# The first stage of a fused two-layer network on one NeuronCore: another order of loads, statistics and roots

## What is computed

```python
x = x + fourier_conv(_ln_c(x))      # layer 0: DFT over axes 1 and 2 (channel, height), 32x32 kept modes,
                                    # a 64x64 complex matrix over the width for each mode, inverse DFT
t = tokens(x); t = t + top2_of_8_experts(_ln_t(t))
x = x + depthwise_29x29_conv(_ln_c(x))   # layer 1
t = tokens(x); t = t + top2_of_8_experts(_ln_t(t))

def _ln_c(v, eps=1e-06):            # normalises each pixel over its 64 channels
    m = mean(v, axis=1); s = var(v, axis=1)
    return (v - m) / sqrt(s + eps)
```

## Time and profile before

| what | value |
|---|---|
| time, median of 3 runs | 1081.36 us (1080.91 to 1082.05) |
| the profiled execution | 1083.87 us, of which 1082.1 us are the span from its first to its last instruction |
| busy, share of the span | PE 82%, DVE 76%, POOL 55%, ACT 49% |
| mean granted TensorE clock | 0.924 of full |
| first stage (input DFT over both axes) | about 0 to 92 us |
| DMA share in 0 to 92 us | 0.82 of the 16 DMA engines, 310 GB/s |

### The profile page before, as it was taken

The page is one execution under the profiler, slowest core; times in us unless marked ns, Lnnn a source line. Parts: engine busy times, 40 slices in busy tenths (PEclk is TensorE's granted clock), DMA queues, the critical chain, the costliest instruction groups (busy, mean ns, idle before and its releaser), DMA issues.

```text
span 1082.1 us, 26559 instructions
## 1 busy us (share of the span) xinstructions
PE 889.9 (82%) x9514; PEld 720.5 (67%) x9514; DVE 824.0 (76%) x1974; ACT 532.4 (49%) x1100; POOL 598.0 (55%) x564
## 2 busy tenths in 40 slices
PE   2994559965799999988469999999726999999987
PEld 2994558864566666655269999999714666666655
DVE  7746976687988898899956777775457988887783
ACT  1446865468466666610034444444158666666400
POOL 1852000052888888777374444440065888888876
PEclk9997559996999999999879999999956999999999
DMA  9895710002499999200358877778100100001100
GB/s 388 312 354 98 186 31 2 2 2 46 165 395 395 397 397 382 97 1 1 134 173 281 270 264 263 268 262 283 47 1 1 41 21 40 39 19 41 40 39 39
DMA packets 53007, 168.22 MB, mean 155 GB/s; under 512 B 13632, under 2 KB 13888, under 8 KB 51136
## 3 DMA queue, kind: packets, MB, share of 16 engines
q1 hardware_dynamic: 52928, 167.19, 43.6%
HBM read 98.68 MB, written 68.49 MB: 154 GB/s over the span
## 4 chain that ended last, share of the span: by engine, by line
PE 32%; POOL 31%; issue 15%; DVE 12%; ACT 5%; DMA 3%; POOLq 1%; SPq 0%; DVEq 0%; ACTq 0%
PE pair L1479 21%; POOL R L530 16%; POOL R L540 9%; PE pair L1383 4%; DVE R L854 2%; DVE R L751 2%; DMA X<-x_rows 2%; DVE work L672 2%; PE pair L1434 2%; POOL R L415 2%; DMA R<-spec_re 1%; ACT pair L1141 1%; PE pair L1431 1%; PE pair L1494 1%; DVE R L775 1%
## 5 line engine op out<-in xcount | busy, mean ns | idle before, releaser
L854 DVE TENSOR_TENSOR R<-pair,R 128x896 f32<-128x896 f32 x256 | 275.9, 1082 | 62.5 <-PE pair L1420 58.2
L530 POOL TENSOR_TENSOR R<-R 128x768 f32<-128x768 f32 x128 | 234.4, 1831 | 90.1 <-DVE R L854 88.4
L1479 PE MATMUL pair<-R 128*128 (+4 forms) x2880 | 227.7, 243 | 19.7 <-DVE R L908 19.7
L1479 PEld LDWEIGHTS pair<-R 128*128 128x128 f16 x2880 | 224.9, 98 | 22.4 <-issue 19.8
L1141 ACT ACTIVATE pair<-X,work 128x64 f32 (+1 forms) x496 | 171.8, 395 | 121.9 <-DVE R L794 116.8
L1419 PE MATMUL pair<-work,R 128*128 128x448 f16 x512 | 185.4, 362 | 46.8 <-DVE R L854 44.3
L1420 PE MATMUL pair<-work,R 128*128 128x448 f16 x512 | 184.5, 360 | 0.0
L540 POOL TENSOR_TENSOR R<-R 128x512 f32<-128x512 f32 x128 | 163.3, 1276 | 12.7 <-POOL R L530 5.2
L917 DVE COPY R<-R 128x1152 f32<-128x1152 f32 x64 | 91.3, 1428 | 78.8 <-PE pair L1479 77.9
L1206 ACT COPY R<-R 128x1152 f32<-128x1152 f32 x64 | 82.0, 1283 | 126.1 <-PE pair L1479 126.1
L1434 PE MATMUL pair<-R,ident_sb 128*128 128x256 f32 x512 | 133.6, 384 | 0.0
(11 more groups left out here) (135 smaller groups left out, 1486.0 us busy)
## 6 DMA issues: line engine op xcount, KB each, us to landing
taps_halves<-R SPq DMA_DIRECT2D x128, 458.5 KB, 6.0
R<-taps_halves SPq DMA_DIRECT2D x64, 917.0 KB, 4.7
R<-spec_re SPq DMA_DIRECT2D x34, 256.0 KB, 4.2
R<-x_chan SPq DMA_DIRECT2D x4, 2048.0 KB, 29.3
X<-x_tok SPq DMA_DIRECT2D x4, 2048.0 KB, 18.1
out<-X SPq DMA_DIRECT2D x16, 512.0 KB, 2.6
X<-x_rows SPq DMA_DIRECT2D x3, 2048.0 KB, 20.0
X<-x_rows SPq DMA_DIRECT2D x2, 1024.0 KB, 5.9
```

The source lines that it names most:

```text
L530: pool.tensor_tensor(pr[:, :, 192:384], pr[:, :, 0:192], pr[:, :, 192:384], ALU.add).then_inc(half_ready, 1)
L854: dve.tensor_tensor(pr.rearrange("p t (e c) -> p t e c", c=C), pair[p % 2][:, :].rearrange("p (t e c) -> p t e c", t=2, c=C)[:, :, 0:NE - ...
L1479: mm = pe.matmul(acc[:, y0:y1, x0:x1, :], blocks[i % 2][:, ks, 2 - y, 1 - x, :], src[:, y0 + y:y1 + y, x0 + x:x1 + x, :], start=(ks == 0 a ...
```

## The change

- **Loads.** The first 1 MB of `x_rows` is followed (after the small `dft` and `rank`) by the first 1 MB of `x_chan`, with a semaphore of its own, `xb_first_in`; then by the second halves of both pieces 0; then rows and channel pieces alternate. TensorE starts step 0 on the first half of piece 0 and waits for the second half at n = 4.
- **Roots in six units** in place of four: (piece 0, halves 1 and 2), (piece 1, halves 1 and 2), piece 2, piece 3. The ten steps of a unit are those of before on 32 or 64 columns. Units 0 and 1 are made before the loop; 2, 3, 4, 5 at n = 3, 7, 13, 21 on GpSimd, always behind the low part of step n-1. Scaling and centring wait for their unit at n = 0, 4, 8, 12, 16, 24 (`UNIT_AT`).
- **Statistics.** VectorE does those of piece 0 ahead of the loop, 32 groups of piece 1 after scaling 3 and 32 after scaling 7, then in steps 8 to 15 those of piece 2 and in steps 16 to 23 those of piece 3: 12 groups after each of the first four scalings, 4 after each of the last four.
- SP waits for six units instead of four pieces before it loads `x_tok`.

```diff
--- before.py
+++ after.py
@@ -166,6 +166,7 @@
         dft_in = sem("dft_in")
         rank_in = sem("rank_in")
         first_in = sem("first_in")
+        xb_first_in = sem("xb_first_in")
         xb_in = [sem(f"xb_in{i}") for i in range(4)]
         xr_in = [sem(f"xr_in{i}") for i in range(4)]
         x_in = sem("x_in")
@@ -273,7 +274,9 @@
         PW = W // 2
         PC = PW * BP * C
         PIECE_STEPS = 10
-        ROOT_AFTER = {3: 1, 7: 2, 15: 3}
+        UNITS = ((0, 0, 32), (0, 32, 64), (1, 0, 32), (1, 32, 64), (2, 0, 64), (3, 0, 64))
+        UNIT_AT = {0: 0, 4: 1, 8: 2, 12: 3, 16: 4, 24: 5}
+        ROOT_AFTER = {3: 2, 7: 3, 13: 4, 21: 5}
         HALF_PAIRS = ((0, 0), (0, 1), (1, 0))
 
         BLOCKS = (slice(0, 64), slice(64, 128))
@@ -317,15 +320,15 @@
 
             half_piece = PC // 2
             sp.dma_start(X[:, 0:half_piece], x_rows[:, 0:half_piece]).then_inc(first_in, 16)
-            sp.dma_start(X[:, half_piece:PC], x_rows[:, half_piece:PC]).then_inc(xr_in[0], 16)
             sp.dma_start(dft_sb[:, :], dft).then_inc(dft_in, 16)
             sp.dma_start(rank_sb[:, :], rank).then_inc(rank_in, 16)
-            sp.dma_start(X[:, piece(1)], x_rows[:, piece(1)]).then_inc(xr_in[1], 16)
-            sp.dma_start(xb[:, piece(0)], x_chan[:, piece(0)]).then_inc(xb_in[0], 16)
-            sp.dma_start(X[:, piece(2)], x_rows[:, piece(2)]).then_inc(xr_in[2], 16)
-            sp.dma_start(xb[:, piece(1)], x_chan[:, piece(1)]).then_inc(xb_in[1], 16)
+            sp.dma_start(xb[:, 0:half_piece], x_chan[:, 0:half_piece]).then_inc(xb_first_in, 16)
+            sp.dma_start(X[:, half_piece:PC], x_rows[:, half_piece:PC]).then_inc(xr_in[0], 16)
+            sp.dma_start(xb[:, half_piece:PC], x_chan[:, half_piece:PC]).then_inc(xb_in[0], 16)
+            for i in (1, 2):
+                sp.dma_start(X[:, piece(i)], x_rows[:, piece(i)]).then_inc(xr_in[i], 16)
+                sp.dma_start(xb[:, piece(i)], x_chan[:, piece(i)]).then_inc(xb_in[i], 16)
             sp.dma_start(X[:, piece(3)], x_rows[:, piece(3)]).then_inc(xr_in[3], 16)
-            sp.dma_start(xb[:, piece(2)], x_chan[:, piece(2)]).then_inc(xb_in[2], 16)
             sp.dma_start(dft16_sb[:, :], dft16).then_inc(const_in, 16)
             sp.dma_start(xb[:, piece(3)], x_chan[:, piece(3)]).then_inc(xb_in[3], 16)
             sp.dma_start(inv_h_sb[:, :], inv_h).then_inc(const_in, 16)
@@ -352,7 +355,7 @@
                     sp.dma_start(k_raw[a % 3][r], spec_re[:, a, 0:16, :]).then_inc(k_in[a % 3], 16)
                 if a == 2:
 
-                    sp.wait_ge(piece_measured, NPIECE)
+                    sp.wait_ge(piece_measured, len(UNITS))
                     for i in range(4):
                         n = NT * C // 4
                         sp.dma_start(X[:, i * n:(i + 1) * n], x_tok[:, i * n:(i + 1) * n]).then_inc(x_in, 16)
@@ -414,12 +417,14 @@
                 out_, src, high_ = low_columns(n)
                 pool.tensor_tensor(out_, src, high_, ALU.subtract).then_inc(c_dft_low, 1)
 
-            def piece_root(i):
+            def unit_root(i):
 
                 base = i * PIECE_STEPS
-                stats = piece_stat[i % 2]
-                shift, root = small[i % 2], small[2 + i % 2]
-                total, gap, spread, t, seed = small[4:9]
+                piece, g0, g1 = UNITS[i]
+                at = slice(g0, g1)
+                stats = piece_stat[piece % 2][:, at, :]
+                shift, root = small[piece % 2][:, at], small[2 + piece % 2][:, at]
+                total, gap, spread, t, seed = (m[:, 0:g1 - g0] for m in small[4:9])
 
                 def step(n):
                     pool.wait_ge(piece_step, base + n)
@@ -432,15 +437,15 @@
                 step(2)
                 pool.tensor_tensor(spread, gap, spread, ALU.add).then_inc(piece_step, 1)
                 step(5)
-                pool.tensor_tensor(total, total, minus_half_c.to_broadcast([P, 64]), ALU.mult)
+                pool.tensor_tensor(total, total, minus_half_c.to_broadcast([P, g1 - g0]), ALU.mult)
                 pool.tensor_tensor(t, seed, seed, ALU.mult).then_inc(piece_step, 1)
                 step(6)
                 pool.tensor_tensor(t, t, gap, ALU.mult).then_inc(piece_step, 1)
                 step(7)
-                pool.tensor_tensor(t, t, three_halves.to_broadcast([P, 64]), ALU.add).then_inc(piece_step, 1)
+                pool.tensor_tensor(t, t, three_halves.to_broadcast([P, g1 - g0]), ALU.add).then_inc(piece_step, 1)
                 step(8)
-                if i >= 2:
-                    pool.wait_ge(c_dft_centred, 8 * (i - 1))
+                if piece >= 2:
+                    pool.wait_ge(c_dft_centred, 8 * (piece - 1))
                 pool.tensor_tensor(root, seed, t, ALU.mult).then_inc(piece_step, 1)
                 step(9)
                 pool.tensor_tensor(shift, total, root, ALU.mult).then_inc(piece_step, 1)
@@ -448,23 +453,22 @@
             def centre_columns(n):
 
                 pool.wait_ge(c_dft_scaled, n + 1)
-                if n % 8 == 0:
-                    pool.wait_ge(piece_step, (n // 8 + 1) * PIECE_STEPS)
+                if n in UNIT_AT:
+                    pool.wait_ge(piece_step, (UNIT_AT[n] + 1) * PIECE_STEPS)
                 at = scaled[n % 4].rearrange("p (g k) -> p g k", k=NJ)[:, :, 0]
                 shift = small[n // 8 % 2][:, 8 * (n % 8):8 * (n % 8) + 8]
                 pool.tensor_tensor(at, at, shift, ALU.add).then_inc(c_dft_centred, 1)
 
             pool.wait_ge(rank_in, 16)
-            piece_root(0)
+            unit_root(0)
+            unit_root(1)
             for n in range(33):
                 if n < 32:
                     centre_columns(n)
-                    if n in ROOT_AFTER:
-                        if n > 3:
-                            c_dft_low_part(n - 1)
-                        piece_root(ROOT_AFTER[n])
-                        if n > 3:
-                            continue
+                if n in ROOT_AFTER:
+                    c_dft_low_part(n - 1)
+                    unit_root(ROOT_AFTER[n])
+                    continue
                 if n == 0 or low_by_vector(n - 1):
                     continue
                 n -= 1
@@ -680,17 +684,17 @@
                 elif lo == 0 or (i == 0 and lo == 32):
                     dve.wait_ge(xr_in[i], 16)
                 if i >= 2 and lo == 0:
-                    dve.wait_ge(piece_step, (i - 2) * PIECE_STEPS + 1)
+                    dve.wait_ge(piece_step, (2 * i - 3) * PIECE_STEPS + 1)
                 for g in range(lo, hi):
                     last = dve.bn_stats(piece_stat[i % 2][:, g, :], xr[:, i * 64 + g, :])
-                if hi == 64:
+                if hi == 64 or (i < 2 and hi == 32):
                     last.then_inc(piece_measured, 1)
 
             def scale_columns(n):
 
                 i, g = n // 8, n % 8
-                if g == 0:
-                    dve.wait_ge(piece_step, (i + 1) * PIECE_STEPS - 1)
+                if n in UNIT_AT:
+                    dve.wait_ge(piece_step, (UNIT_AT[n] + 1) * PIECE_STEPS - 1)
                 dve.wait_ge(c_dft, n + 1)
                 if n >= 4:
                     wait_c_dft_low(dve, n - 3)
@@ -719,11 +723,13 @@
 
             piece_stats(0, 0, 32)
             piece_stats(0, 32, 64)
-            piece_stats(1, 0, 64)
             for n in range(32):
                 scale_columns(n)
-                if n < 16:
-                    piece_stats(2 + n // 8, 8 * (n % 8), 8 * (n % 8) + 8)
+                if n in (3, 7):
+                    piece_stats(1, 8 * n - 24, 8 * n + 8)
+                if 8 <= n < 24:
+                    i, g = n // 8 + 1, n % 8
+                    piece_stats(i, 12 * g if g < 4 else 32 + 4 * g, 12 * g + 12 if g < 4 else 36 + 4 * g)
                 if n >= 18 and low_by_vector(n - 1):
                     c_dft_low_part(n - 1)
                 if n >= 24:
@@ -1025,10 +1031,10 @@
                         bank[4 + n % 4][:, 0:na * 68].rearrange("p (a k) -> p a k", a=na), DOWN1
                         ).then_inc(h_dft_high, 1)
 
-            def piece_seed(i):
+            def unit_seed(i):
 
                 base = i * PIECE_STEPS
-                gap, spread, t, seed = small[5:9]
+                gap, spread, t, seed = (m[:, 0:UNITS[i][2] - UNITS[i][1]] for m in small[5:9])
                 act.wait_ge(piece_step, base + 1)
                 act.activation(gap, gap, ACT.Square, scale=4.0).then_inc(piece_step, 1)
                 act.wait_ge(piece_step, base + 3)
@@ -1039,11 +1045,12 @@
 
             act.preload_act_table_set("natural_log_exp_and_others")
             act.wait_ge(rank_in, 16)
-            piece_seed(0)
+            unit_seed(0)
+            unit_seed(1)
             for n in range(32):
                 c_dft_high_part(n)
                 if n in ROOT_AFTER:
-                    piece_seed(ROOT_AFTER[n])
+                    unit_seed(ROOT_AFTER[n])
                 if n >= 24:
```

(4 more changed lines are left out.)

## The result

The changed kernel takes 1086.1 us (median of 17 runs), the kernel before 1082.9 in the 17 runs beside it: ratio 1.003, 95% interval 1.0018 to 1.0043, or 1.9 to 4.7 us slower. One of the 17 runs of the changed kernel took 1354.5 us at a mean granted clock of 0.66; ratio and interval leave it out, and the median moves by less than 0.1 us without it. The profiled execution of the changed kernel took 1085.9 us with a span of 1084.1, against 1083.87 and 1082.1.

A forecast was written before the change was run, and what follows sets the result against it. The prediction took the chain of statistics, roots and ring, not TensorE, to end the first stage: 2.6 us later, plus 1.4 for a lower clock, so 1081.4 + 4.0 = 1085.4 us; range 1081.6 to 1087.8.

The forecast's parts named there:

- the chain of statistics, roots and ring: First stage, VectorE and GpSimd with ScalarE: runs beside TensorE's own chain and ends last, at 85.2 us before the change.
- the ring: First-stage loop: scaling, centring, cast, high and low part of `dft_over_h`, VectorE and ScalarE waiting for each other; 2.255 us a step.
- closing block: TensorE's last matmuls of the first stage, after a pause; from 85.2 to 91.2 us before the change.
- the rival of TensorE's start: First stage: if the vector side could follow, the loop begins and ends 10.8 us earlier, 1070.6; chance 0.07.
- The loads: Start of first stage: TensorE begins at 8.3 us, 10.8 earlier; piece 1's rows are complete at 19.0 instead of 13.3.
- the rival of later loads: First stage: alternating pieces land 2 us late, +2.0 on top, 1087.4; chance 0.10 shared with a wholly slow block.
- TensorE's stalls: First-stage loop: waits of 1.7, 2.7, 1.4 and 2.8 us and smaller ones eat TensorE's lead; loop finished at 79.7.
- The chain: First stage, VectorE and GpSimd: scaling 7 at 28.5, 16 at 48.6, 24 at 67.5, 25 at 71.35; stage 2.6 us later.
- Both roots stood open: First stage, roots 4 and 5 on GpSimd: VectorE idles 4.7 us ahead of each of scalings 16 and 24.
- The rival of cheaper open roots: First stage: roots 4 and 5 begin when GpSimd is free; +1.1 us for scaling 24, 1082.5 with clock up; chance 0.13.
- The clock: End of first stage: clock falls in TensorE's 7.8 us pause, closing block loses 1.4 us, bounds 0 to 3.6.
- Behind the stage: After the first stage: nothing is late, later loads are down in time, and everything shifts with the stage's end.

The follow-up runs named there:

- kernel with early fill: Kernel with all follow-up edits together, plus 26 float16 matmuls on constants while TensorE waits for its first data, against that kernel; ratio to before 0.9922.
- filled pause: Changed kernel plus 16 unread float16 matmuls in TensorE's pause ahead of the closing block, against the changed kernel; ratio to before 1.0011.

## Why the prediction was right, and where it was off

The forecast was 4.0 us slower, the measured difference 3.2 (1.9 to 4.7).

- *What bounds.* Right: the chain of statistics, roots and ring ends the stage. Cutting the ring by itself took 3.5 us off the start of the closing block in the kernel before and 6.8 in the changed one, and the edit that starts TensorE 2.5 us later changed nothing. That answers the rival of TensorE's start too, with the changed loads alone, which started it 10 us earlier and ended the stage 4.7 us later.
- *The loads.* TensorE's start was put at 8.3 and came at 9.04 (8.84 to 9.65 in the kernels with this order of loads); rows' second half at 10.75 and came at 11.38. The small tables between the loads may have cost more than I allowed; no run shows it. Neither is on the chain. Piece 1's rows are, and they came 0.25 us late (19.25 for 19.0), not the 2 us of the rival of later loads. TensorE's stalls were each some half a microsecond shorter than worked out (1.1, 2.2, 0.9 and 2.2 us for 1.7, 2.7, 1.4 and 2.8), and it was through with the loop at 79.8 (79.7 forecast).
- *The chain.* Scaling 7 at 28.58 (28.5 forecast), 16 at 48.50 (48.6), 24 at 67.27 (67.5), 25 at 71.28 (71.35). The root of 32 columns held GpSimd 4.0 us (15.61 to 19.61), as that of the tokens did; the root of 64 columns 4.8. Both roots stood open for 4.54 us (4.7 forecast). The stage: 2.56 later, 2.6 forecast.
- *The rival of cheaper open roots* has its test in GpSimd's waits of 0.87 and 1.35 us ahead of roots 4 and 5: the statistics were late, as worked out.
- *The clock* is the step that was wrong. I took 1.4 us for a fall in a pause of 8 us, and read TensorE at its full clock from 20 to 80 us. There was no higher level to fall from: it was at the lower one already, before and after the change, and the block took 5.93 and 5.94 us. The fall behind the stage that I reasoned from the earlier trace rows is real (94.43), but from a level that the record has only from 91.01 on, 0.15 us before the block's end; nothing had been held across the pause of 4.9 us. The pace could have told: the same pace over 60 us of full work and on both sides of a pause, under a record without a single change. The term should have been 0, and so 2.6 us for the whole, inside the interval. That the interval holds 4.0 as well is luck and no support for the term; the 0.6 us between 2.6 and the measured 3.2 it can't tell from nothing.
- *Behind the stage* nothing took the 2.6 us up or added to it that can be told from the 2 us by which that rest varies.

The one open point: TensorE's level rose 2.8 to 5.9 us after the closing block's start, between kernels whose stage is alike, and the block took 4.75 to 5.94 us accordingly. What decides on early or late isn't shown; only one execution of each kernel has a trace. It is a possible 1.2 us for either kernel. The two traces compared here both have the late rise, so their 2.56 us are free of it, but the comparison of medians contains it.

## What to carry to other kernels

A transfer that lands earlier is worth what the next engine's next wait leaves of it: follow the instruction streams to the stage's end before counting it, for here a start 10 us earlier came out 2.6 us late. Where two engines wait for each other within each step of a loop, the ring's latency is its pace; moving one instruction a step later was worth more than all the loads. An open wait isn't lost time as long as the engine has the same work to do anyway: giving it other work there moved the end by a fraction of the wait, and the wait turned up elsewhere.

## What the runs showed of the hardware that I had not expected

- The granted clock of the windows is 1.00 until the record's first entry, also where TensorE is at the lower level: steps of 1.72 us stand under "1.00" in the kernel before and under "0.50" in the kernel with early fill, where the same step took 0.92 at the real higher level. In all 14 traces the first entry is a stretch at 1.00, and in the 12 where TensorE works on behind its start the pace rises there.
- Float32 steps kept TensorE busy without a gap for over 40 us in the kernel before, and steps and pairs together for 61, and the level did not rise. In the fill of float16 matmuls of 512 columns it rose 1.9 us after the start in the two kernels where TensorE had been at work right up to the fill, and 6.0 in the one where it had done nothing before; afterwards the float32 steps kept the level for 7.3 us in one kernel and, with the pairs, for 11.7 in another. It fell 4.2 us after the last fill matmul in the filled pause, and 2.5 us after TensorE stopped at 18.6 in the kernel with early fill.
- TensorE: Matmul & The Clock Gate, Part 1, in the Trainium skill, calls the half rate the default from which activity lifts the array. The runs agree (0.43 us each for the first fill matmuls, 0.92 for 1.72 us a step after them); the printed 1.00 at the start does not show it. That 61 us of busy TensorE in the kernel before did not lift it, the sentence leaves open.
